# Re-timing the side network of a two-layer gated cross-attention kernel: three score banks, half a bank for weighed values, VectorE pieces one later

## The reference

```
x = x + tanh(g_xattn[0]) * cope_attention(layernorm(x), ctx)   # 16 heads of 16; CoPE position term per head
x = x + tanh(g_ffn[0])   * expert_ffn(layernorm(x))            # 8 experts, top 2, and one shared expert
x = x + tanh(g_xattn[1]) * cross_attention(layernorm(x), ctx)  # 16 heads
x = x + tanh(g_ffn[1])   * gated_attention(layernorm(x))       # 16 heads, normalized queries, gated heads
```

## Time and profile before

| | |
|---|---|
| Median of three runs | 5371.37 us |
| The profiled execution, its own time | 5382.85 us |
| Its span, first to last instruction | 5381.1 us |
| VectorE busy | 3956.2 us (74%) |
| TensorE busy, weight loads | 3448.0 us (64%), 2230.8 us (41%) |
| ScalarE busy | 2431.1 us (45%) |
| GpSimd busy | 1386.8 us (26%) |

### The profile page before, as it was taken

The page is one execution under the profiler, slowest core; times in us unless marked ns, Lnnn a source line. Parts: engine busy times, 40 slices in busy tenths (PEclk is TensorE's granted clock), DMA queues, the critical chain, the costliest instruction groups (busy, mean ns, idle before and its releaser), DMA issues.

```text
span 5381.1 us, 64444 instructions
## 1 busy us (share of the span) xinstructions
PE 3448.0 (64%) x21126; PEld 2230.8 (41%) x21126; DVE 3956.2 (74%) x8619; ACT 2431.1 (45%) x5441; POOL 1386.8 (26%) x1125
## 2 busy tenths in 40 slices
PE   3447575665757667575665757667575665757576
PEld 2225253443525335253443625335353443525353
DVE  3688686786867768686786867778687776867753
ACT  2454444444444444444444444444444454444432
POOL 0342223223222222223223222222222222222300
PEclk7558686776857768586776857768686776857777
DMA  4000000000000000000000000000000000000000
GB/s 122 8 5 1 3 9 1 11 1 10 1 1 11 1 10 1 3 9 1 11 1 10 1 1 11 1 10 1 2 9 1 11 1 10 1 1 7 1 7 3
DMA packets 42690, 40.91 MB, mean 8 GB/s; under 512 B 6468, under 2 KB 42342, under 8 KB 42360
## 3 DMA queue, kind: packets, MB, share of 16 engines
q1 hardware_dynamic: 42360, 36.85, 2.2%
HBM read 32.64 MB, written 4.19 MB: 7 GB/s over the span
## 4 chain that ended last, share of the span: by engine, by line
DVE 37%; PE 35%; ACT 12%; issue 11%; POOL 2%; POOLq 0%; ACTq 0%; DVEq 0%; DMA 0%; SPq 0%
PE banks L786 6%; DVE banks L710 5%; DVE row_negmax L1220 5%; PE banks L355 5%; PE banks L264 4%; PE banks L286 4%; DVE masks L701 3%; PE banks L799 3%; DVE steps L726 3%; PE banks L319 3%; DVE u L937 2%; DVE c L672 2%; PE banks L1088 2%; PE banks L277 2%; DVE eg_eth L955 2%
## 5 line engine op out<-in xcount | busy, mean ns | idle before, releaser
L710 DVE COPY_PREDICATED banks<-masks,banks 128x448 f32<-128x448 int16 (+5 forms) x1536 | 1029.4, 670 | 31.7
L615 POOL TENSOR_TENSOR steps<-slope,rises 128x512 f32<-128x512 f32 x256 | 303.0, 1183 | 2900.4 <-DVE masks L701 2524.2
L786 PE MATMUL banks<-xn,w 128*128 128x256 f16 x6912 | 878.7, 288 | 167.7 <-ACT h L858 165.4
L786 PEld LDWEIGHTS banks<-xn,w 128*128 128x128 f16 x6912 | 700.3, 104 | 342.1 <-ACT h L858 195.2
L701 DVE TENSOR_SCALAR masks<-shift 128x512 int16<-128x512 int16 x1536 | 335.0, 289 | 473.1 <-ACT shift L543 469.2
L582 ACT ACTIVATE core_pT<-banks 128x512 f32<-128x512 f32 x256 | 152.9, 597 | 616.7 <-PE banks L264 616.1
L799 PE MATMUL banks<-w,a 128*128 128x256 f32 x1152 | 326.4, 434 | 141.7 <-DVE o L964 141.7
L629 POOL TENSOR_TENSOR partial<-partial,core_scores 128x512 f32<-128x512 f32 x256 | 350.6, 1369 | 0.1
L1220 DVE TENSOR_REDUCE row_negmax<-banks 128x4 f32<-128x1024 f32 x256 | 302.9, 1219 | 58.4 <-PE banks L340 58.4
L672 DVE TENSOR_TENSOR_SCAN c<-gate,cap 128x514 f32<-128x514 f32 x256 | 342.0, 1336 | 1.1 <-ACT gate L527 1.1
L1088 PE MATMUL banks<-eg_eth,h 64*128 64x256 f16 x1024 | 253.2, 367 | 127.5 <-ACT a L1155 85.2
(11 more groups left out here) (262 smaller groups left out, 7349.4 us busy)
## 6 DMA issues: line engine op xcount, KB each, us to landing
stage<-in_L_ffn_w SPq DMA_DIRECT2D x16, 512.0 KB, 5.5
...
```

Source lines behind the costliest of these rows:

```text
L710: move = nc.vector.copy_predicated(tab[:, :, 0:S - b], k.masks[:, n, :, 0:S - b], tab[:, :, b:S])
L786: last = nc.tensor.matmul(k.bank[bank][:, f * S:(f + 1) * S], w[:, e, a, c, par, f * P:(f + 1) * P], k.x_parts[:, b, c, :], start=(n == 0) ...
```

## The change

- Transposed scores go to bank 5 + h % 3, so TensorE waits for the exp of head h - 3 and no longer h - 2.
- `weigh_four` of all groups writes half g % 2 of bank 4. From g = 2 on it waits for the copy of group g - 2. ScalarE copies a group of 256 columns at a time, the first three behind the exps of heads 6, 10 and 14, the last at the end.
- VectorE pieces that take a TensorE or ScalarE product move one piece later than the piece that makes it: `add_to_x` after the first block joins the layer norm's piece, the last `accumulate` of the expert block moves a piece, the second part of the queries too. The cross attention's projection of keys and values gets a piece apart from the query projection. The gated attention's preparation is cut into seven pieces, of which three are empty on TensorE and ScalarE.
- `PIECE_TIMES` is new, for 110 pieces and no longer 106, and the ahead pieces start one slot later (`AHEAD`, 16 pieces, the value copy L657 in the one behind its product).

The pieces dealt to slots 3, 4, ..., 15, 0, 1, 2 are 4 3 4 3 4 3 4 3 20 12 4 3 4 21 11 3 before and 4 3 4 4 3 4 4 6 19 10 4 4 11 16 10 4 after; `FIRST` is 3 2 3 2 3 2 3 2 13 8 3 2 3 14 7 2 before and 3 2 3 3 2 3 3 4 13 7 3 3 7 11 7 3 after. So after the change all 18 first products stand in slots 4 to 8. Slot 9 has the last down product, the cross projections, and slot 10 both stacks and scores of heads 0 to 3. Slot 11 has heads 4 to 15, the maxima and transposed heads 0 to 5, slot 12 transposed heads 6 to 15, slot 13 the end of cross, slot 14 the gated projections and key stacks. Slot 15 has the query stacks and heads 0 to 7, slot 0 heads 8 to 15, the maxima and transposed heads 0 to 6, slot 1 heads 7 to 15 and the last weighing, slot 2 the end.

```diff
-PIECE_TIMES = [4] * (4 + 2 * NE) + [2] * 2 + 2 * ([6] * 4 + [0.5] * (H + 1) + [1.2] * (H + 1) + [5] * 3)
+PHASES = [0.5] * (H + 1) + [1.4] * (H + 1)
+PIECE_TIMES = [4] * (4 + 2 * NE) + [2] * 2 + [6] * 4 + PHASES + [5] * 3 + [3.5] * 7 + PHASES + [4] * 4
-AHEAD = [1, 0, 0, 1, 2] + [1] * (H - 5)
+AHEAD = [1, 1, 0, 1, 1, 2] + [1] * (H - 6)
...
 side_vector:
     yield
+    yield
     dve.wait_ge(sem["tail_y_done"], at["tail_y_done"] + 1)
     dve.wait_ge(sem["loads"], at["loads"] + 16 * 2 * NT)
     add_to_x(nc, k, step, k.bank[7], k.tanh_g[:, 0:1], k.bo_cope)
-    yield
     norm_vector(nc, k, dve, step, k.norm, "ffn_", at)
...
+    yield
     accumulate(NE - 1)
     step(nc.vector.scalar_tensor_tensor(whole(k.norm.x), whole(k.acc), k.tanh_g[:, 2:3], whole(k.norm.x),
                                         ALU.mult, ALU.add))
-    yield
     yield
...
 attention_tensor:
     if kind == "cross":
         keys_and_values(k.ctxT)
+    yield
     pe.wait_ge(sem[p + "xn_ready"], at[p + "xn_ready"] + NT)
     transpose_tokens(nc, k, k.bank[4], n.xn).then_inc(sem[p + "xT_psum"], 1)
-    yield
     pe.wait_ge(sem[p + "xT_ready"], at[p + "xT_ready"] + 1)
...
     if kind == "gated":
+        yield
+        key_stacks()
+        yield
+        yield
         pe.wait_ge(sem[p + "q_done"], at[p + "q_done"] + 1)
         transpose_tokens(nc, k, k.bank[4], k.qn).then_inc(sem[p + "qT_psum"], 1)
+    else:
+        key_stacks()
     yield
...
         pe.wait_ge(sem[p + "pT_ready"], at[p + "pT_ready"] + 4 * g + 4)
-        weigh_four(nc, k.v, HD + 1, k.pT, g, k.bank[4 + g // 2], g % 2).then_inc(sem[p + "pv_done"], 1)
+        if g >= 2:
+            pe.wait_ge(sem[p + "oH_ready"], at[p + "oH_ready"] + g - 1)
+        weigh_four(nc, k.v, HD + 1, k.pT, g, k.bank[4], g % 2).then_inc(sem[p + "pv_done"], 1)
...
     for h in range(H):
-        if h >= 2:
-            pe.wait_ge(sem[p + "pT_ready"], at[p + "pT_ready"] + h - 1)
+        if h >= 3:
+            pe.wait_ge(sem[p + "pT_ready"], at[p + "pT_ready"] + h - 2)
...
-            out = k.bank[6 + h % 2][:, c * S:(c + 1) * S]
+            out = k.bank[5 + h % 3][:, c * S:(c + 1) * S]
...
 attention_scalar:
+    def values(g):
+        act.wait_ge(sem[p + "pv_done"], at[p + "pv_done"] + g + 1)
+        nc.scalar.activation(k.oH[:, g, :], k.bank[4][:, g % 2 * S:(g % 2 + 1) * S], ACT.Copy)\
+            .then_inc(sem[p + "oH_ready"], 1)
+
...
-    for n in range(2):
-        act.wait_ge(sem[p + "pv_done"], at[p + "pv_done"] + (n + 1) * H // 8)
-        nc.scalar.activation(whole(k.oH[:, 2 * n:2 * n + 2]), k.bank[4 + n][:], ACT.Copy)\
-            .then_inc(sem[p + "oH_ready"], 1)
+        if h >= 6 and h % 4 == 2:
+            values((h - 6) // 4)
+        yield
+    values(H // 4 - 1)
     yield
```

More of the change, by code:

```diff
@@ L120, in ahead_pieces @@
 def ahead_pieces(s):
-    return AHEAD[s % H] if s >= 4 and s < G + 4 else 0
+    return AHEAD[s % H] if s >= 5 and s < G + 5 else 0
 def raised_by(b):
@@ L599, in ahead_pool @@
     norm_pool(nc, k, pool, k.core_norm, "core_", raised_by(b))
-    for _ in range(14):
+    for _ in range(15):
         yield
@@ L653, in ahead_vector @@
     yield
-    for _ in range(9):
+    for _ in range(10):
         yield
@@ L903, in side_pool @@
                 .then_inc(k.sem[p + "rnorm_ready"], 1)
-        for _ in range(3 + 2 * H + 5):
+        for _ in range((5 if kind == "gated" else 3) + 2 * H + (6 if kind == "gated" else 5)):
             yield
@@ L1031, in keys_and_values, with key_stacks @@
         token_projection(nc, w.wv, src, k.bank[6]).then_inc(sem[p + "v_psum"], 1)
+    def key_stacks():
+        pe.wait_ge(sem[p + "k_second"], at[p + "k_second"] + NC)
+        pe.wait_ge(sem[p + "v_ready"], at[p + "v_ready"] + 1)
+        for m in range(P // HB):
+            if m >= 2:
+                pe.wait_ge(sem[p + "k_stack"], at[p + "k_stack"] + m - 1)
+            stack_pair(nc, k, 1, k.k_parts, m, k.bank[5 + m % 2]).then_inc(sem[p + "k_stack_psum"], 1)
     if kind == "cross":
         keys_and_values(k.ctxT)
+    yield
     pe.wait_ge(sem[p + "xn_ready"], at[p + "xn_ready"] + NT)
     transpose_tokens(nc, k, k.bank[4], n.xn).then_inc(sem[p + "xT_psum"], 1)
-    yield
     pe.wait_ge(sem[p + "xT_ready"], at[p + "xT_ready"] + 1)
@@ L1121, in keys, with key_stacks @@
         first_part(nc, k.bank[5], w.bk, k.k_parts, sem[p + "k_first"])
+    def key_stacks():
+        for m in range(P // HB):
+            copy_stacks(nc, act, m, k.bank[5 + m % 2], k.keys, sem[p + "k_stack_psum"], sem[p + "k_stack"],
+                        at[p + "k_stack_psum"])
     if kind == "cross":
         keys()
+    yield
     act.wait_ge(sem[p + "xT_psum"], at[p + "xT_psum"] + 1)
     nc.scalar.activation(whole(k.norm.xT), k.bank[4][:], ACT.Copy).then_inc(sem[p + "xT_ready"], 1)
-    yield
     if kind == "gated":
@@ L1133, in attention_scalar @@
     yield
-    for m in range(P // HB):
-        copy_stacks(nc, act, m, k.bank[5 + m % 2], k.keys, sem[p + "k_stack_psum"], sem[p + "k_stack"],
-                    at[p + "k_stack_psum"])
     if kind == "gated":
+        yield
+        key_stacks()
+        yield
+        yield
         act.wait_ge(sem[p + "qT_psum"], at[p + "qT_psum"] + 1)
         first_part(nc, k.bank[4], None, k.q_parts, sem[p + "q_first"])
+    else:
+        key_stacks()
     yield
     for m in range(P // HB):
-        copy_stacks(nc, act, m, k.bank[7 - 3 * (m % 2)], k.queries, sem[p + "q_stack_psum"], sem[p + "q_stack"],
-                    at[p + "q_stack_psum"])
+        copy_stacks(nc, act, m, k.bank[7 - 3 * (m % 2)], k.queries, sem[p + "q_stack_psum"],
+                    sem[p + "q_stack"], at[p + "q_stack_psum"])
     yield
@@ L1197, in attention_vector @@
     last.then_inc(sem[p + "v_ready"], 1)
-    if kind == "cross":
-        dve.wait_ge(sem[p + "q_first"], at[p + "q_first"] + NC)
-        second_part(nc, k.bank[7], w.bq, k.q_parts, sem[p + "q_second"])
     yield
     if kind == "gated":
+        yield
         heads = k.qn.rearrange("p t (h d) -> p (t h) d", d=HD)
```

27 lines of the change are left out of this document (15 added, 12 removed).

## The result

The changed kernel takes 5251.83 us (median of four runs, 5250.48 to 5252.24), the kernel before 5371.19 beside it: 0.9771 of before, interval 0.9753 to 0.9789. That is 119 us less; 80 were forecast. Its profiled execution is one of the four (5251.89, span 5250.2).

A forecast was written before the change was run, and what follows sets the result against it. No engine alone bounds the kernel: work is handed round, VectorE idling 77.3 of 321.2 us per batch. Slot terms sum to 5.1 less per batch; 15 batches give -76, the last -4, so 5291 us, own range 5235 to 5345.

The forecast's parts named there:

- Slots 3 and 15: Slot 3 from 23.9 to 19.3 us by later add_to_x and core_v; slot 15 from 20.3 to 24.3 by three more pairs.
- Slots 4 to 8: The expert slots, full on both sides: 97.9 to 101.6 us for one more expert piece and core_v.
- Slot 10: Both stacks and heads 0 to 3: 14.8 to 17.8 us, with a new VectorE wait of 5.9.
- Slot 9: Loses an expert piece and the expert-sum wait, gets second keys part and value copy: 23.1 to 16.6 us.
- Slots 11, 12, 0, 1: Maxima and transposed scores: 22.1 to 23.4, 19.7 to 18.7, 23.4 to 22.1 and 20.8 to 20.4 us.
- Slots 13 and 14: Cross end and gated preparation: 37.9 to 35.4 us, less add_to_x waiting, slot 14 ending by ScalarE's copies as before (+0.9).
- Slot 2: End of the gated attention: 17.3 to 16.5 us, as the routing waits less.
- The last side: Last batch's side, without core work: third bank and copies save 4 us, from bank waits of 0.7 and 1.2 twice.
- A: Rival: clock holds in slots 11, 12, 0 and 1, 5.4 us more saved per batch, 5205 us; chance 0.13.
- B: Rival: waits displaced from slots 3, 9 and 13 to four others, net -0 to -1, 5365 us; chance 0.12.
- C: Rival: slots 10, 11, 15 and 0 grow more than forecast, +8, so +3 per batch, 5416 us; chance 0.20.

The follow-up runs named there:

- e3: Changed kernel with both add_to_x, last expert sum, query part, gated routing and core_v back in their products' pieces; dealing, cuts, banks kept: 5385.5 us, 0.9994 of before.
- e5: Changed kernel with each pair of row maxima reduced two pieces behind its scores: 5213.38 us, 0.9705 of before.
- e7: Kernel before with only the first add_to_x, core_v and the ahead pieces moved later: 5372.51 us, 1.0004 of before.
- e6: Kernel before with all later VectorE places and later ahead pieces; banks, weights and cuts as before: 5299.59 us, 0.9852 of before.
- e4: Changed kernel with transposed heads reordered so that nearly all neighbours use the same 64 TensorE rows: 5258.5 us, 0.9767 of before.
- e1: Changed kernel with transposed scores back on two banks, half bank and copies kept: 5261.81 us, 0.9775 of before.
- e8: Kernel before with three banks, half bank, copies and all later VectorE places, but old weights and cuts: 5289.95 us, 0.9847 of before.
- e11: e8 with a transposed head weighing 1.4 instead of 1.2, so pieces stand nearly as in the changed kernel: 5199.55 us, 0.9671 of before.
- e2: Kernel before with only the three banks, half bank and copies of the change: 5316.79 us, 0.988 of before.
- e10: e5 with transposed scores on two banks instead of three: 5252.59 us, 0.9771 of before.

## Why the prediction was right, and which steps were not

The direction and the mechanism held: waits went where VectorE's pieces moved, new ones came where products and consumers met, and the sum was a gain. Terms of both signs were mis-sized: four promised too much, by 1.2 to 3.1 us (6.9 in all), six too little (10.1 in all), and the sum of changes came to -8.4 us per batch for -5.1 (up to 0.8 of it is the slower profiled execution of before). That errors of both signs offset one another was luck.

- **Slots 3 and 15.** Changes of -4.6 and +4.0 forecast, -5.0 and +3.1 measured. e3 gives slot 3 back when the deferral goes, e5 gives 1.7 of slot 15 back when the maxima come later: waits removed and waits made were both on the path. What `core_v` still waits for its product (18.7 us) is one single wait in the run.
- **Slots 4 to 8.** +3.7 forecast, +3.6 measured, with other parts than mine: e7, without any new expert piece, has 1.2 of it. Of e7's moved pieces, those in these slots are the ahead pieces. A whole list was moved by a slot and I priced only `core_v` of it; its product L406 stands ahead of slot 10 in e7.
- **Slot 10.** +3.0 forecast, +4.2 measured, but the length is the forecast one, 17.8, and the wait for the maxima is the 5.9 that was forecast. The base differs: the forecast started from a batch with 14.8 at a clock of 0.62, and most batches had 13.1 at 0.76.
- **Slot 9.** -6.5 forecast, -5.2 measured. The wait for the expert sum went (50.2 to 2.2), but e3, with the sum in its old place, has 2.2 too (its trace, the same line), and e6, with the later sum in the old dealing, 27.8. The new dealing takes the wait away alone, the later `accumulate` only half of it.
- **Slots 11, 12, 0, 1.** -1.4 forecast, -10.2 measured: the large miss. The starts were right: the first of the maxima was packed 11.2 into slot 11 (11.5 forecast), the weighing started 6.2 into slot 12 (6.5). The packing, in the slot that starts at 2089.8:

```profile
2101.03 0.18 DVE L1260 CAST small<-row_negmax 128x64 bf16<-128x64 f32 x1
```

  What followed was shorter. The windows from that weighing to the slot's end, slots 12 and 1, before and after:

```profile
2163.90:2178.00 14.10, 11.17 (x100) 5.13 (x100) 3.89 (x8) 7.38 (x14) 0.88 (x1) 0.73 0.01 1
...
2265.20:2280.40 15.20, 11.78 (x92) 5.04 (x96) 3.77 (x7) 7.63 (x15) 0.80 (x1) 0.61 0.00 1
```
```profile
2117.70:2128.00 10.30, 7.60 (x72) 3.90 (x72) 3.27 (x7) 6.25 (x13) 0.10 (x1) 0.83 0.01 2
...
2217.30:2228.40 11.10, 8.22 (x84) 4.02 (x76) 3.15 (x7) 6.32 (x13) 0.00 (x0) 0.89 0.00 0
```

  The granted clock there is 0.83 and 0.89 for 0.73 and 0.61; in slot 12 I had taken the middle between no rise and a rise half way, and in slot 1 none. And each head was charged 0.85 of TensorE, where neighbours overlap. The overlap alone is worth 1.1 per batch in these slots by e4, the third bank 1.2 by e1 (1.4 forecast). e8, with banks and deferral but the old dealing, has only 2.0 of the 10.2, so most of it comes with the new dealing. The batches at other clocks bound the clock's part. Slots 11 and 0 stand at 0.50 before and after, so their 3.4 is no clock. At equal clocks slot 1 is 2.0 shorter in e3 than before (0.50), and slot 12 2.7 shorter (17.8 for 20.5, both at 0.60). That leaves some 2 of the 10.2 to the clock, an estimate from these rows. How the other 8 split between overlap and fewer pieces ahead of `slope` isn't settled.
- **Slots 13 and 14.** -2.5 forecast, +0.6 measured. That the slot "ends by ScalarE's copies as late as before" was the wrong step: the three preparation pieces stand ahead of the core's transposes, so `slope` waits for all of them. With four pieces (e11) the change is -2.6.
- **Slot 2.** -0.8 forecast, +0.5 measured. By e3 the deferral is worth 1.5 there and the new dealing costs 2.0; the second part was not in my term. Part of it is the clock again: the changed kernel has 17.0 in seven batches, at 0.75 to 0.76, and 18.4 to 18.8 in the others, at 0.66 to 0.67.
- **The last side** gave 10.0 for 4: e2's banks and copies give 6.0 of it, e8 8.6. The parts named in that term (four waits of 0.7 and twice 1.2) add up to 5.2, and not 4.

The rivals. A (clock holds in all four slots, 5205) is wrong for slots 11 and 0, at 0.50, and half right for 12 and 1. Did the clock rise because the bank waits went? e1 has 113.7 us of such waits, the changed kernel 10.0, and e1 has the same mean clock in slot 12 (0.69 for 0.70) and a higher one in slot 1 (0.79 for 0.72). e10 against e5 has it lower in slot 12 (0.59 for 0.66) and higher in slot 1 (0.75 for 0.71). Here the clock didn't follow the bank waits in any steady way. The Trainium skill ("TensorE: Matmul & The Clock Gate", section "A second HAM failure mode: psum-queue depth-cycling") tells of a kernel that cycles through banks, idles in small gaps and so swings between two clocks; by that a rise was to be expected once the gaps were gone, and in three of these four pairs it didn't come. B (waits displaced) is what e7's time shows for slot 3 by itself; with dealing and deferral together it is wrong. C needed 5.1 more than I gave in slots 10, 11, 15 and 0; their changes came out 3.1 less.

The account by parts: deferral alone -1.5%, banks and copies alone -1.2%, both together -1.5%, dealing with cuts and banks but no deferral 0. My reading is that each removes one link of a chain that is then closed elsewhere, and the clock moves with it. Together with the dealing of e11 they give -3.3%. The change left 1.0% of that behind, by its finer cuts and the dealing that came with them; slot 14's 3.1 us are the part that the timelines show.
